# Two linear layers with a mask and a low-rank part on one core: the first layer by halves of its outputs, 512-column matmuls in it

## The reference

```
x: (8, 256, 1024) fp32; mask: (8, 1024, 1024) int32
# layer 0
output = einsum('bsi,oi->bso', x, W0) + b0
diff   = einsum('bsi,bio->bso', x, 2 * mask - 1)
x      = x + output + diff * coeff[b]
# layer 1
base   = einsum('bti,oi->bto', x, W1) + b1
lora   = einsum('btr,bro->bto', einsum('bti,bir->btr', x, A[slot[b]]), B[slot[b]])
x      = x + base + lora * 2.0
```

## Time and profile before

| | |
|---|---|
| median of 3 runs | 395.39 us (395.38 to 395.57) |
| the profiled execution | 395.45 us |
| its span, first to last instruction | 393.6 us |
| TensorE busy, matmul | 385.2 us, 98% |
| DVE busy | 221.9 us, 56% |
| ACT busy | 160.1 us, 41% |
| granted TensorE clock, mean | 0.999 of full speed |

### The profile page before, as it was taken

How to read it: one execution, slowest core, us unless ns; L and a number is a source line. 1 busy time by engine, 2 the same in 40 slices (tenths; PEclk the granted TensorE clock), 3 DMA queues, 4 the chain that set the end, 5 groups by cost and what they waited for, 6 DMA issues and landing times.

```text
span 393.6 us, 6757 instructions
## 1 busy us (share of the span) xinstructions
PE 385.2 (98%) x2782; PEld 382.8 (97%) x2782; DVE 221.9 (56%) x267; ACT 160.1 (41%) x283; POOL 39.9 (10%) x44
## 2 busy tenths in 40 slices
PE   8799999999999999999999999999999999999997
PEld 8798999999999999999999999999999999999996
DVE  3898989568470765527753476515846168461200
ACT  3447844264331643235432552316524064332311
POOL 2335600020000200002000020000100020000200
PEclk9999999999999999999999999999999999999999
DMA  8999726814741165602665035631365315300111
GB/s 287 410 396 356 303 79 247 296 55 159 233 172 60 64 211 182 190 31 81 215 215 167 2 124 196 231 124 55 104 223 188 109 53 184 113 0 2 54 55 53
DMA packets 20912, 61.80 MB, mean 157 GB/s; under 512 B 2554, under 2 KB 3730, under 8 KB 20882
## 3 DMA queue, kind: packets, MB, share of 16 engines
q1 hardware_dynamic: 18064, 52.70, 38.3%
q10 hardware_dynamic: 2754, 8.66, 6.2%
q0 software_dynamic: 64, 0.01, 0.0%
HBM read 52.97 MB, written 8.39 MB: 156 GB/s over the span
## 4 chain that ended last, share of the span: by engine, by line
PE 90%; DMA 5%; SPq 2%; DVE 1%; issue 1%; POOL 0%; ACT 0%; DVEq 0%; ACTq 0%
PE z_ps L320 45%; PE y_ps L296 27%; PE y_ps L306 14%; DMA w_raw<-in_w 2%; DMA w_t<-in_w 2%; PE y_ps L320 2%; PE z_ps L364 2%; DVE wc_lo L589 1%; PE t_ps L355 0%; POOL w_t L232 0%; DVE ring L580 0%; SPq L173 0%; SPq L179 0%; SPq L176 0%; SPq L183 0%
## 5 line engine op out<-in xcount | busy, mean ns | idle before, releaser
L320 PE MATMUL z_ps<-w_hi,y_two 128*128 128x344 f32 (+1 forms) x736 | 183.7, 323 | 1.0 <-DVE y_two L612 1.0
L296 PE MATMUL y_ps<-x_two,wc_hi 128*128 128x256 f32 x1024 | 133.6, 283 | 1.5 <-ACT wc_hi L425 1.5
L320 PEld LDWEIGHTS z_ps<-w_hi,y_two 128*128 128x128 f32 x736 | 129.4, 188 | 1.8 <-issue 1.1
L296 PEld LDWEIGHTS y_ps<-x_two,wc_hi 128*128 128x128 f32 x1024 | 127.7, 192 | 1.8 <-DVE x_two L605 1.7
L320 PE MATMUL z_ps<-w_lo,y_two 128*128 128x344 f32 (+1 forms) x368 | 118.2, 321 | 0.0
L589 DVE SCALAR_TENSOR_TENSOR wc_lo<-ring,coeff_neg,wc_hi 128x1024 fp32r<-128x1024 f32 (+1 forms) x65 | 82.7, 1274 | 41.0 <-ACT wc_hi L425 40.4
L425 ACT ACTIVATE wc_hi<-ring,coeff_neg 128x1024 fp32r<-128x1024 f32 (+1 forms) x65 | 74.0, 1139 | 59.0 <-PE y_ps L306 43.3
L580 DVE SCALAR_TENSOR_TENSOR ring<-ring,coeff_two,w_t 128x1024 f32<-128x1024 int32 (+1 forms) x65 | 83.4, 1291 | 7.5 <-DMA ring<-in_mask 6.7
L306 PE MATMUL y_ps<-x_two,wc_lo 128*128 128x256 f32 x512 | 72.3, 284 | 1.5 <-DVE wc_lo L589 1.3
L320 PEld LDWEIGHTS z_ps<-w_lo,y_two 128*128 128x128 f32 x368 | 69.3, 188 | 0.0
L306 PEld LDWEIGHTS y_ps<-x_two,wc_lo 128*128 128x128 f32 x512 | 65.9, 192 | 2.3 <-DVE wc_lo L589 2.3
(11 more groups left out here) (35 smaller groups left out, 92.1 us busy)
## 6 DMA issues: line engine op xcount, KB each, us to landing
ring<-in_mask SPq DMA_DIRECT2D x63, 512.0 KB, 3.4
x_raw<-in_x SPq DMA_DIRECT2D x31, 256.0 KB, 4.9
out<-z_rows ACTq DMA_DIRECT2D x15, 512.0 KB, 2.9
w_raw<-in_w SPq DMA_DIRECT2D x8, 512.0 KB, 10.1
w_t<-in_w SPq DMA_DIRECT2D x7, 512.0 KB, 8.0
b_raw<-in_lora_b SPq DMA_DIRECT2D x8, 256.0 KB, 3.5
w_t<-in_w SPq DMA_DIRECT2D x2, 256.0 KB, 3.7
ring<-in_mask SPq DMA_DIRECT2D x2, 256.0 KB, 4.7
```

The costliest lines, as they stand in the source:

```text
L296: pe.matmul(ys, w, x_two[:, k, n, :], start=(k == 0 and o % PAIR == 0 and n == 0), stop=False, skip_group_check=True)
L320: ins = pe.matmul(z_bank(b, s, g)[:, 0:EDGES[g + 1] - EDGES[g]], ys[:, k, s * P:(s + 1) * P], w[:, k, EDGES[g]:EDGES[g + 1]], start=(k == ...
```

## The change

Batch 0 stays block by block, with two differences: its first three blocks (`HALVED = 3`) are made and used in two halves of 512 outputs, and output 1 adds up in `t_ps` in place of sharing `y_ps0` (`first_bank`). DVE makes the low part of output 0 as soon as ACT has rounded output 0.

From batch 1 on layer 0 runs in two halves of four outputs. A unit u (0 to 7) holds two blocks k and the 512 outputs of one half: units 0 to 3 are half 0, 4 to 7 half 1. Loads, ring slots, sums and roundings go by units, with as many elements as a block had (`unit`, `slot`, mask rows of 2 KB). Each output has a whole bank: one matmul of 512 columns takes `wc_hi` by x's high and low part together, into 512 columns of the bank, and `wc_lo` by x's high part adds to its first 256. ACT copies the second 256 with the bias to `y_raw` (`y_copy`), DVE adds the first 256 (`y_sum`), then ACT rounds and DVE subtracts two outputs at a time (`y_high`, `y_low`). `y_two` is single now. TensorE: half 0, `layer1_last` of the batch before, half 1, then layer 1, whose groups of s = 0 begin with their first four k, all three of them.

```diff
-            def layer0(b):
-                for k in range(KT):
-                    layer0_high(b, k)
-                    layer0_low(b, k)
+            def bank_free(b, o):
+                if b == 1 and o < HT:
+                    pe.wait_ge(y_lo_done, PAIR * (o + 1))
+                    if o < 2:
+                        pe.wait_ge(z_done, z_place(0, 1, o))
+                else:
+                    pe.wait_ge(y_sum_done, KT * (b - 1) + o + 1 - HT)
+            def unit_high(b, u, k, o):
+                if k == 0:
+                    bank_free(b, o)
+                w = slot(wc_hi, u)[:, k % PAIR, (o % HT) * P:(o % HT + 1) * P]
+                pe.matmul(y_ps[o % HT][:, 0:2 * T], w, x_two[:, k, :, :], start=(k == 0), stop=False,
+                          skip_group_check=True)
+            def unit_low(b, u, k, o):
+                w = slot(wc_lo, u)[:, k % PAIR, (o % HT) * P:(o % HT + 1) * P]
+                ins = pe.matmul(y_ps[o % HT][:, 0:T], w, x_two[:, k, 0, :], start=False, stop=(k == KT - 1),
+                                skip_group_check=True)
+                if k == KT - 1:
+                    ins.then_inc(y_full, 1)
+                return ins
+            def layer0_half(b, h):
+                for u in range(HT * h, HT * (h + 1)):
+                    pe.wait_ge(x_lo_done, XG * b + u % HT + 1)
+                    pe.wait_ge(wc_hi_done, parts(b, u))
+                    for k in range(PAIR * (u % HT), PAIR * (u % HT + 1)):
+                        outs = range(HT * h, HT * (h + 1))
+                        if k == KT - 1:
+                            sets = [[o] for o in outs]
+                        elif (b, u, k) == (1, 0, 0):
+                            sets = [outs[2:4], outs[0:2]]
+                        else:
+                            sets = [outs]
+                        for part in sets:
+                            for o in part:
+                                unit_high(b, u, k, o)
+                            pe.wait_ge(wc_lo_done, parts(b, u))
+                            for o in part:
+                                ins = unit_low(b, u, k, o)
...
             for b in range(1, NB):
-                layer0(b)
+                layer0_half(b, 0)
                 layer1_last(b - 1)
+                layer0_half(b, 1)
                 layer1(b)
...
+            def first_bank(o):
+                return t_ps[:, 0:T] if o == 1 else y_ps[o // PAIR][:, (o % PAIR) * T:(o % PAIR + 1) * T]
...
             def layer1(b):
+                for g in range(NG):
+                    layer1_group(b, 0, g, range(HT))
+                layer1_group(b, 0, 0, range(HT, KT))
+                layer1_group(b, 0, 1, range(HT, KT))
+                turn_h(b, 0)
+                layer1_group(b, 0, 2, range(HT, KT - PAIR))
+                close_group(b, 0, 0)
+                close_group(b, 0, 1)
+                layer1_group(b, 0, 2, range(KT - PAIR, KT))
+                close_group(b, 0, 2)
...
+            def y_copy(b, o):
+                act.wait_ge(y_full, y_count(b, o))
+                if b > 1:
+                    act.wait_ge(y_lo_done, y_split(b - 1, o))
+                act.activation(y_raw[:, o, :], y_ps[o % HT][:, T:2 * T], ACT.Identity,
+                               bias=b0_cols[:, o:o + 1]).then_inc(y_copied, 1)
...
+            def y_sum(b, o):
+                dve.wait_ge(y_copied, KT * (b - 1) + o + 1)
+                dve.tensor_tensor(y_raw[:, o, :], y_ps[o % HT][:, 0:T], y_raw[:, o, :],
+                                  ALU.add).then_inc(y_sum_done, 1)
```

More of the change, by code:

```diff
@@ L125, in cond_residual_two_layers, with unit, slot @@
         mask_v = mask.rearrange("b (k p) o -> b k p o", p=P)
+        mask_u = mask.rearrange("b (k p) o -> b p k o", p=P)
+        def unit(u):
+            j, h = u % HT, u // HT
+            return slice(PAIR * j, PAIR * (j + 1)), slice(HALF * h, HALF * (h + 1))
+        def slot(buf, e):
+            return buf[:, e % RING, :].rearrange("p (k o) -> p k o", k=PAIR)
         def mask_entry(b, k):
@@ L408, in _ @@
             warm_up(30)
-            layer0(0)
+            for k in range(KT):
+                layer0_high(k)
+                layer0_low(k)
             layer1_first()
             for b in range(1, NB):
-                layer0(b)
+                layer0_half(b, 0)
                 layer1_last(b - 1)
+                layer0_half(b, 1)
                 layer1(b)
@@ L422, in weights_high @@
                 e = mask_entry(b, k)
[L423 removed]
+                for lo, hi in ((0, HALF), (HALF, D)) if b == 0 and k < HALVED else ((0, D),):
                     act.wait_ge(sum_done, parts(b, k, lo // HALF))
@@ L656, in _ @@
             h_low(0, 1)
-            for k in range(KT):
+            for k in range(HT):
                 if k + 1 < XG:
```

262 lines of the change are left out of this document (148 added, 114 removed).

## The result

The changed kernel takes 392.24 us (median of 4 runs, 392.08 to 392.74), the kernel before 395.48 us beside it (395.38 to 395.64): a ratio of 0.992, 95% interval 0.9903 to 0.9937. It is faster, by 3.2 us; the forecast was 6.4 us, and the time lies above the range. The profiled execution took 392.74 us for a span of 390.9 us, half a microsecond above the median, so between the two profiles only 2.7 us are to be found.

A forecast was written before the change was run, and what follows sets the result against it. TensorE, busy 98% of the span, was taken as the bound. 5.97 (merged pairs) + 0.45 (batch 0) = 6.4 us off 393.6 gives a span of 387.2; with 1.85 us around it, 389.0 us, range 387.0 to 391.6.

The forecast's parts named there:

- the faster end: Layer 0's merged matmuls: a fixed cost near nothing, 215.8 ns at 512 columns, would save 10.8 us.
- the main term: Layer 0, batches 1 to 7: 448 merged pairs each save a fixed surcharge of 13.3 ns, 5.97 us in all.
- outer bound: Layer 0's merged matmuls: if the surcharge went on growing with width, 232.3 ns each and 3.4 us saved.
- Spare 0.8 us: nothing: Layer 1 of batch 1: y's k = 4 ready at 87.4, needed at 88.2, so no wait was counted.
- third step: batch 0: End of batch 0's layer 0: output 1's own bank gains 0.45 us, between 0 and 0.7; halved blocks count 0.
- what sets that end: Batch 0's layer 0: DVE's low part of block 6 waits behind block 7's sum, POOL's w0 diagonal and its DMA.
- what had to hide: From batch 1 on: bank reads between halves (spare 2.7 us), y for layer 1 (3.2), h's transpose (0.35) cost nothing.
- The bridge: The last layer 1 group of the batch before, run between layer 0's two halves, 3.97 us, covering the bank reads.
- (a): Layer 0's 512-column matmuls pay little surcharge: 10.8 to 12 us saved, 383 to 384 us; chance 0.04.
- (b): Layer 0's merge gives nothing, 240.0 ns per 512 columns; only batch 0's 0.45 stays, 394.9 us; chance 0.04.
- (c): y reaches layer 1 too late through DVE's list in half 1, 2.0 us x 7 = 14 us: 403 us; chance 0.06.
- (d): Inside the forecast's case (0.86): dearer surcharge, up to 391.6 us, or waits of 0.3 us per batch, 391.1.

The follow-up runs named there:

- e_split: The changed kernel with every 512-column matmul put back into two of 256 columns in the same bank: 395.6 us, ratio 0.9997.
- m_width: The changed kernel with eleven blocks of 64 unneeded matmuls appended after layer 1, widths 512 to 128, other engines idle: 227.0 ns per matmul at 512 columns.
- e_bank1: The changed kernel with output 1 of batch 0 back in output 0's bank and DVE waiting for both of ACT's reads: 392.43 us, ratio 0.9911.

## Why the prediction came out as it did

**Right: the mechanism and the direction.** Merging pairs is the gain (e_split gives it all back, to 0.03%). Matmuls of one width pace as the prediction estimated, 227.0 ns for 226.7 (m_width).

For the faster end the prediction had the rule of the Trainium skill (TensorE: Matmul & The Clock Gate, Back-to-back issue gap) for isolated matmuls, N / 2.4 + 2.5 ns: 215.8 at 512 columns. No run agrees; the sweep has 10.7 to 13.5 ns more at every width from 256 to 512. The same section states some 131 ns for 512 columns in a stream of weight loads and matmuls, and the sweep, with 227.0, does not show that either.

**Wrong, first step: the main term.** "I take 13.3: same weights' buffers, same x tile, same stage." 448 pairs were to give 5.97 us, and gave 7 x 0.57 = 4.0. The prediction took the low matmuls at 120 and the high ones at 226.7; measured are 118.3 and 232.5, a pair of 350.8 against 346.7. A half takes 7 x 1403 + 1410 ns = 11.23 us instead of 11.09; 14 halves lose 1.9 us. No row of before could show it: layer 0 had one width, layer 1 two that are 8 columns apart, in long runs. That 232.3 ns, the prediction's own outer bound, is near the measured 232.5 is luck: it stood for a surcharge that grows with the width, and m_width rules that out. The range ended there (3.4 us) with the gain in batch 0 added and no wait beside it.

**Wrong, second step: batch 1.** "Spare 0.8 us: nothing" was put in the sum, and the wait was 0.99 us. The list of DVE was right in order and nearly in time: the third low part was to end at 85.1, and ended at 87.8, 2.1 of it by the one long step. But the list left out POOL. In the kernel before, `lora_b_low` of batch 1 ran at 86.27, when DVE was idle for all but its end, and took 2.38 us. In the new order it falls into DVE's densest stretch. The full price stood in the trace of before once, in batch 0; a small part of it stood in batches 1 to 6, where the sum that DVE began just before POOL's end took 1.50 to 1.77 us in place of 1.28. DVE, then POOL, of the kernel before:

```profile
44.10 5.68 DVE L600 TENSOR_TENSOR w_lo<-w_raw,w_hi 128x1024 fp32r<-128x1024 f32 x3
...
45.33 3.36 POOL L248 TENSOR_TENSOR b_stack<-b_raw,b_stack 32x1024 fp32r<-32x1024 f32 x1 [1.77 <-ACT b_stack L479]
...
86.27 2.38 POOL L248 TENSOR_TENSOR b_stack<-b_raw,b_stack 32x1024 fp32r<-32x1024 f32 x1 [25.60 <-ACT b_stack L479]
```

The third of the three steps, from 46.37 to 49.78, takes 3.41 us where the two ahead of it take 1.13 each from start to start. The prediction did not use this row. It had named the size ("if each step there slipped by 10% it would cost about 1 us, once") and kept it as an end of the range, but as general slip, not as this clash.

**Wrong, third step: batch 0.** +0.45 us was forecast. The bank's part came nearly whole (0.36 us, from e_bank1), but layer 0 of batch 0 ended later in the profiled execution (last matmul's start 35.74 for 35.00), so that profile has -0.34. The prediction was right on what sets that end: POOL's diagonal behind the DMA of w0's last block, and it came at 27.82 us instead of 26.83. It had no term for this arrival moving, which it does by up to 1.1 us from profile to profile (26.82 to 27.88), more than the whole gain forecast. Over eleven profiles the median start of layer 1 is that of before. The mask's shorter rows are not the cause, since batch 0 loads whole blocks in both kernels. Whether the block really lands later in the changed kernel, or the one profile of before was an early one, no run decides.

The sum by its steps: 6.4 - 1.9 (pace) - 1.0 (wait) - 0.8 (batch 0) = 2.7 us between the profiles; the median, 0.5 us below the profiled execution, makes 3.2 of it.

**Right: what had to hide.** The bridge is 3.97 us as in the earlier trace rows, and no half waits for a bank; h's transpose hides behind six matmuls; the mask's shorter rows cost no wait; DVE in batches 2 to 7 is in time, though it meets the clash in batches 2 to 6 as well. The rivals (a), (b) and (c) did not occur as they stood, (c) having the wait in every batch. Of (d), which was counted inside the forecast, the dearer surcharge came, and beside it one wait of 1.0 us in place of tenths per batch. Pace and wait alone, 4.0 - 1.0 = 3.0 us, give 392.4 by the prediction's own base of 395.4, and that is outside the range already.

## What to carry to other kernels

Merging two matmuls of the same weights saves their fixed surcharge once per pair, but a pace read from a stream of one width need not hold in a mix of widths: here a third of the saving was lost so, and longer runs of one width gave part of it back. When an edit moves one engine's work in time, look also at engines it never waits for: here DVE's dense stretch came to lie over a POOL instruction that had run beside a nearly idle DVE. A spare of 0.8 us is none where the same trace shows a step of that engine 2 us over its usual length.
